# Attention outputs that stay channel-major: transposes on TensorE against a trip through DRAM

## The reference

```python
# L0: RWKV-like mix (shift, two causal scans, sigmoid gate), then one selected 128x128 linear
# L1_attn: 16 heads of 8 channels, full attention over 512 tokens
# L1_ffn:  mixture of 8 experts (hidden 176, top 2) plus a shared one
# L2_attn: 16 heads, rotary, causal
# L2_ffn:  rmsnorm, rotary causal attention with 16 query and 4 key heads, rmsnorm,
#          mixture of 8 experts (hidden 256, top 2)
# L3_attn: 16 query and 4 key heads, causal with ALiBi slopes
# L3_ffn:  layernorm, ternary-quantized 128 -> 512, gelu, layernorm, 512 -> 128
scores = jnp.einsum('bhqd,bhkd->bhqk', Q, K) * scale
attn = jax.nn.softmax(scores, axis=-1)
out = jnp.einsum('bhqk,bhkd->bhqd', attn, V)
out = out.transpose(0, 2, 1, 3).reshape(B, N, D)
return out @ wo.T
```

## Time and profile before

| | us |
|---|---|
| median of 3 runs | 1389.61 |
| lowest and highest | 1388.29, 1390.61 |
| the profiled execution | 1386.62 |
| its span | 1384.8 |
| TensorE busy | 1218.0 (88%) |
| VectorE busy | 932.8 (67%) |
| ScalarE busy | 710.5 (51%) |
| GpSimd busy | 269.9 (19%) |
| mean granted TensorE clock | 0.949 |

### The profile page before, as it was taken

One profiled execution on the slowest core, in us unless ns is written; L12 is line 12 of the kernel. 1 busy time (PEld: TensorE's weight loads), 2 busy tenths in 40 slices (PEclk: granted clock), 3 DMA queues, 4 the chain that ended last, 5 costly groups with the idle time before them and its releaser, 6 DMA issues.

```text
span 1384.8 us, 26785 instructions
## 1 busy us (share of the span) xinstructions
PE 1218.0 (88%) x8190; PEld 650.1 (47%) x8190; DVE 932.8 (67%) x2502; ACT 710.5 (51%) x1300; POOL 269.9 (19%) x557
## 2 busy tenths in 40 slices
PE   3446999999889998999999999999999979999876
PEld 1222233333356655445555555556666535455445
DVE  5877778687455555767778776755554476668676
ACT  2221776777644434566666666663222227666643
POOL 3342211111000012322332332110000211222112
PEclk7557999999999998999999999999999989999988
DMA  7312232310000003323333222100000202221000
GB/s 207 124 65 73 87 90 68 120 35 19 1 1 1 0 1 120 105 66 107 106 98 126 74 78 76 45 4 3 1 0 0 74 12 67 77 81 40 2 1 31
DMA packets 65200, 79.16 MB, mean 57 GB/s; under 512 B 5483, under 2 KB 58068, under 8 KB 64602
## 3 DMA queue, kind: packets, MB, share of 16 engines
q1 hardware_dynamic: 65098, 77.89, 18.1%
HBM read 45.27 MB, written 31.72 MB: 56 GB/s over the span
## 4 chain that ended last, share of the span: by engine, by line
PE 62%; issue 13%; DVE 9%; ACT 4%; DMA 4%; DVEq 3%; POOL 2%; SPq 1%; POOLq 1%; ACTq 0%
PE bank L1606 11%; PE bank L1620 11%; PE bank L1590 9%; PE bank L1772 6%; PE bank L1773 6%; PE bank L1790 5%; PE bank L1574 3%; PE bank L1608 2%; DVE M L1189 2%; DMA KS<-scr_k 2%; PE bank L1640 2%; DVE masked_scores L1186 1%; PE bank L1510 1%; DVE N L1026 1%; PE bank L1570 1%
## 5 line engine op out<-in xcount | busy, mean ns | idle before, releaser
L912 ACT ACTIVATE PT<-bank 128x512 f32<-128x512 f32 (+1 forms) x784 | 427.5, 569 | 246.9 <-PE bank L1608 176.2
L1590 PE MATMUL bank<-KS,QS 125*128 125x512 bf16 (+3 forms) x1024 | 308.6, 329 | 31.5 <-DVE M L1186 12.1
L1606 PE MATMUL bank<-QS,KS 128*128 128x512 bf16 (+3 forms) x1024 | 303.7, 323 | 15.2 <-ACT PT L912 8.0
L1189 DVE TENSOR_REDUCE M<-bank 128x1 f32<-128x512 f32 (+2 forms) x400 | 257.8, 684 | 87.9 <-PE bank L1590 52.2
L1186 DVE CUSTOM_DVE_ANT_0 masked_scores<-bank,maskw 128x384 bf16<-128x384 f32 (+1 forms) x384 | 228.7, 622 | 90.0 <-PE bank L1590 78.8
L1620 PE MATMUL bank<-PT,VA 128*32 128x512 f32 (+3 forms) x2048 | 211.5, 485 | 1.6 <-ACT PT L912 1.0
L1606 PEld LDWEIGHTS bank<-QS,KS 128*128 128x128 bf16 x1024 | 99.3, 98 | 215.5 <-ACT PT L912 152.4
L1590 PEld LDWEIGHTS bank<-KS,QS 125*128 125x128 bf16 x1024 | 100.6, 99 | 109.0 <-DVE M L1189 31.9
L1608 PE MATMUL bank<-identb,maskw 128*128 128x128 bf16 x768 | 147.7, 219 | 0.0
L1790 PEld LDWEIGHTS bank<-MW,PT 128*128 128x128 f32 x864 | 111.7, 193 | 40.8 <-issue 38.2
L1772 PE MATMUL bank<-XT,MW 128*128 128x512 f32 (+1 forms) x232 | 120.7, 602 | 10.1 <-DVE PT L1363 5.9
(11 more groups left out here) (229 smaller groups left out, 1522.6 us busy)
## 6 DMA issues: line engine op xcount, KB each, us to landing
scr_q<-PQ SPq DMA_DIRECT2D x48, 384.0 KB, 3.2
QS<-scr_q SPq DMA_DIRECT2D x64, 288.0 KB
scr_k<-PK SPq DMA_DIRECT2D x24, 384.0 KB, 3.6
KS<-scr_k SPq DMA_DIRECT2D x32, 288.0 KB
QS<-MSB SPq DMA_DIRECT2D x192, 4.0 KB
MW<-in_m_w SPq DMA_DIRECT2D x3, 1024.0 KB, 9.5
MW<-in_m_w SPq DMA_DIRECT2D x3, 832.0 KB
scr_k<-PK SPq DMA_DIRECT2D x24, 96.0 KB, 1.9
```

What stands on the lines that cost most here:

```text
L912: a.activation(PT[kt % 2][:, js[0]:js[-1] + 1, q0:T], tiles(bank[st_bank(L, g, i)][:, 0:w * len(js)], len(js)), ACT.Exp, scale=c["scale"]) ...
L1189: v.tensor_reduce(M[g % 2][:, t * GH + js[0]:t * GH + js[-1] + 1], tiles(bank[S_ORDER[L][i]][:, 0:kl * len(js)], len(js)), AX_X, ALU.max, ...
L1590: r = mm(s, QS[0:ROWS_SHIFT, g * GH + j, t * P:(t + 1) * P], KS[0:ROWS_SHIFT, kv_slot(L, g, j), 0:kl], start=True, stop=not by_pe)
L1606: r = mm(s, KS[:, kv_slot(L, g, j), kt * P:(kt + 1) * P], QS[:, g * GH + j, T - w:T], start=True, stop=not causal)
```

## The change

The output of a unit is never transposed. SP stores `OT` (256 KB) of each unit to a DRAM scratch, `scr_o`, as soon as ScalarE has copied it. When the four units of a block are stored, SP loads the block back twice: the 128 channel rows to `OU`, and the 16 rows of sums, each spread to the 8 rows of its head, to `OS`. VectorE inverts `OS` in place in four pieces of 128 columns, at items 0 to 3 of g=1 in the next block. GpSimd multiplies `OU` with `OS` to `AOT`, and the product with `wo` follows at item 7 of g=1. `o_t`, `o_norm`, `ao_t` and `ao_out` are gone.

```diff
+LAST_R_AT = {2: (0, 1), 3: (2, 3)}
+LAST_Y_AT, LAST_SUM_AT, LAST_NORM_AT, LAST_XT_AT, LAST_OUT_AT = 5, 5, 7, 8, 8
...
-SHIFT_T_AT, O_OUT_AT, O_T_AT, O_NORM_AT, AO_T_AT, AO_OUT_AT = 3, 3, 6, 7, 9, 10
-Y_AT, Y_SUM_AT, Y_STATS_AT = (1, 1), (1, 4), (1, 6)
+SHIFT_T_AT, O_OUT_AT = 3, 3
+RECIP_AT = {(1, 0): 0, (1, 1): 1, (1, 2): 2, (1, 3): 3}
+Y_AT, Y_SUM_AT, Y_STATS_AT = (1, 7), (1, 8), (1, 8)
...
-EARLIER = dict(norm=(2, 1), stats2=(2, 1), norm2=(2, 3), xt=(2, 6), out=(2, 7))
+EARLIER = dict(norm=(2, 2), stats2=(2, 2), norm2=(2, 4), xt=(2, 6), out=(2, 7))
...
-LATE_LOGITS_AT, LATE_GATES_AT, LATE_T_AT = 6, 7, 11
+LATE_LOGITS_AT, LATE_GATES_AT, LATE_T_AT = 9, 9, 12
...
+            def store_o(L, b, g):
+                sp.wait_ge(o_evac, U(L, b, g) + 1)
...
+                    at_least(sp, o_landed, (b + NB * L) * 32)
...
+                sp.dma_start(bass.AP(tensor=scr_o, offset=g * P * T, ap=[[T, P], [1, T]]), OT[:, :]).then_inc(o_stored, 16)
+            def load_o(L, b):
+                B = b + NB * L
+                sp.wait_ge(o_stored, (U(L, b, NG - 1) + 1) * 16)
...
+                sp.dma_start(OS[:, :], bass.AP(tensor=scr_o, offset=HD * T, ap=[[32 * T, H], [0, HD], [1, T]])).then_inc(o_landed, 16)
+                sp.dma_start(OU[:, :], bass.AP(tensor=scr_o, offset=0, ap=[[32 * T, H], [T, HD], [1, T]])).then_inc(o_landed, 16)
...
                     if g == 0:
                         load_stack(L, b, 3)
+                    if g >= 2 and ahead:
+                        load_stack(ahead[0], ahead[1], g - 1)
+                    if prev:
+                        store_o(*prev)
                     if follow:
                         load_shift(*follow)
+                    if end and g == 0:
+                        load_o(*end)
                     if prep:
                         store_parts(*prep)
                         load_stack(*prep, 0)
-                    elif g >= 2 and ahead:
-                        load_stack(ahead[0], ahead[1], g - 1)
                 sequence(L, unit, sp.Fori)
+                if ends_chain(L):
+                    store_o(L, NB - 1, NG - 1)
+                    load_o(L, NB - 1)
...
+            def scale_o(L, b):
+                B = b + NB * L
+                wait(recip_done, (B + 1) * NT)
+                wait(y_ready, b + NB * LAYERS[L]["phase"])
+                g.tensor_tensor(AOT[:, :], OU[:, :], OS[:, :], ALU.mult).then_inc(ao_ready, 1)
...
                     if gg == 1 and end:
+                        scale_o(*end)
                         post_root(LAYERS[end[0]]["phase"], end[1])
...
+            ffn_root(0)
+            scale_o(3, NB - 1)
             post_root(L3_ATTN, NB - 1)
-            ffn_root(0)
+            ffn_root(1)
             post_save(L3_ATTN, NB - 1)
-            ffn_root(1)
...
+            def recip(L, b, i):
+                if i == 0:
+                    dve.wait_ge(o_landed, (b + NB * L + 1) * 32)
+                here = OS[:, i * P:(i + 1) * P]
+                v.reciprocal(here, here).then_inc(recip_done, 1)
```

At the ends of the chains: in both mixtures the four reciprocals stand after chunks 2 and 3 of the first block, `y_out` and `post_sum` with `post_stats` at chunk 5 (into bank 7, no longer bank 6), the norm at 7, the transposes of the result at 8, logits at 9, the gate steps at 9, 10 and 11, and both gate transposes at 12. In the last feed-forward, for VectorE:

```diff
                 if b == 0:
-                    post_sum(L3_ATTN, NB - 1)
+                    for i in range(NT):
+                        recip(3, NB - 1, i)
+                elif b == 1:
+                    post_sum(L3_ATTN, NB - 1, bank[7])
                     post_stats(L3_ATTN, NB - 1)
-                elif b == 1:
-                    post_norm(L3_ATTN, NB - 1)
-                    post_stats2(L3_ATTN, NB - 1)
...
                 if b < NB:
                     ffn_stats(b)
                 if b == 1:
+                    post_norm(L3_ATTN, NB - 1)
+                    post_stats2(L3_ATTN, NB - 1)
                     post_norm2(L3_ATTN, NB - 1)
```

141 lines of the change are left out of this document (61 added, 80 removed).

## The result

The changed kernel takes 1408.52 us (median of 4, 1406.51 to 1409.21); the kernel before took 1390.11 on the same chip (1388.29 to 1391.95). The ratio is 1.013, with a 95% interval of 1.0112 to 1.0148: slower, by 18.4 us, where 10.3 were forecast. Its profiled execution took 1406.51 us, with a span of 1404.7, against a span of 1384.8 before.

A forecast was written before the change was run, and what follows sets the result against it. Inside attention TensorE's own work was taken to set the pace. The terms -32.5 + 30.5 - 3.2 + 4.8 + 4.8 - 1.5 + 6.4 + 1 gave +10.3 us: median 1399.9 us, range 1376 to 1417.

The forecast's parts named there:

- TensorE's gain: Inside attention: dropping the transposes of 61 units and 13 blocks, 0.44 us each, saves 32.5 us, as TensorE is full.
- units g=2 and 3 are 0.44 us shorter: Sign to look for in attention: these units shorten by 0.44 us while TensorE idles about 2 us a block at g=1.
- VectorE at g=1: Attention units g=1 of 13 blocks: reciprocals make VectorE lag and TensorE wait for score banks, +30.5 us (13 to 46).
- the 0.1 us for `y_out`'s wait: At item 7 of g=1: the projection waits about 0.1 us more for GpSimd's multiply behind the fourth reciprocal.
- absorbed by the cheap items behind: At item 8 of a causal g=1: the 2.4 us of sum and statistics together would cost nothing more.
- SP: DMA queue: earlier stack loads remove four KS waits, -3.2 us; output stores delay shift rows at four units, +4.8 (0 to 9).
- Mixtures: First mixture loses 4.8 us (0 to 8) through moved VectorE work and transposes behind the gates; the second gains 1.5.
- Feed-forward: Last feed-forward, VectorE setting the pace: late loads, moved statistics and an uncovered GpSimd root delay the second norm, +6.4 us (2 to 9).
- The banks do not absorb it: Rival: score banks absorb VectorE's lag at g=1, 1.0 us a block, total -7.2, 1382 us; chance 0.27.
- Rows late everywhere: Rival: each store delays shift rows past the next unit by 0.5 us in 48 causal units, +24, 1424 us; chance 0.09.
- the two signs of being wrong: In attention: units g=1 growing by less than 1.1 us, or waits for OS standing on VectorE.
- Hidden edges: Rival: feed-forward and mixture keep their time through unseen slack, -11.2, 1389 us, no difference; chance 0.09.

The follow-up runs named there:

- experiment 8: The kernel before with the four transposes of each unit's output done twice, same result: 1404.65 us, ratio 1.0109.
- experiment 4: The kernel before with four unused 128x128 reciprocals added to VectorE at items 0 to 3 of each block-ending g=1: 1413.07 us, ratio 1.0163.
- experiment 5: The changed kernel with the output projection at item 9 of g=1 instead of 7, sum and statistics at item 10 instead of 8: 1420.08 us, ratio 1.0218.
- experiment 10: Changed kernel, projection at item 9, statistics at 10 of g=1, GpSimd's root behind the split, normalizations later, chains' last blocks as in changed kernel: 1400.36 us, ratio 1.0083.
- experiment 1: The changed kernel with each of the four reciprocals of a block inverting only one column: 1371.86 us, ratio 0.9882.
- experiment 7: The changed kernel inverting compact 128x64 sums before spreading in 13 blocks, with later projection and statistics and reordered last feed-forward: 1422.12 us, ratio 1.0229.
- experiment 9: The changed kernel with compact inversion in ten blocks, GpSimd's multiply behind the split, projection at g=2, normalizations at g=3: 1412.95 us, ratio 1.0189.
- experiment 12: The compact inversion in ten blocks with projection at g=2, plus SP's spreading load moved behind the shift rows: 1398.59 us, ratio 1.0066.
- experiment 11: The changed kernel with SP issuing the shift rows ahead of the store of the output in every unit: 1421.99 us, ratio 1.0244.
- experiment 3: The changed kernel with only the order of VectorE's and GpSimd's work in the last feed-forward changed: 1405.70 us, ratio 1.012.
- experiment 2: The kernel before with only SP's stack loads of g=2 and 3 issued ahead of the shift rows: 1382.56 us, ratio 0.9964.

## Why the prediction was right, and where its size was off

The direction and the mechanism held, and 1408.5 lies in the range; but the range, 1376 to 1417, was wide enough to hold a faster kernel too. The sum was 8 us short by the medians (10.3 of 18.4) and 9.7 by the profiles: the units g=1 took 6.7 more than forecast, the feed-forward 1.5, the start 1.4 by scatter. The mixtures nearly cancel. Outside g=1 the total came out within 0.8, by luck: the transposes gave some 6 us less than forecast, and the stores cost some 4 less.

**TensorE's gain: too large by some 6 us.** "TensorE is full there" was read from two units and applied to 61. Experiment 8 adds what two thirds of them would. Outside g=1, the changed kernel won 23.4 us. Of these 3.2 are the KS waits and 0.7 the last block, whose wait of 2.44 for the normalized rows became 1.74 where +1 was forecast; the first block of layer 1 lost 1.0 on MSB. That leaves about 20.5 for the transposes, against 26.8. The sign "units g=2 and 3 are 0.44 us shorter" held at g=3 (0.27 to 0.44, more where a KS wait went too); the 13 units g=2 behind a block's end won 1.3 us together, not 5.7.

**VectorE at g=1: 37 instead of 30.5** (if the transposes gave their 5.7 there). The lag of the reciprocals was sized at 29 (2.2 a causal block); experiment 4 gives 24 by adding them, 1.9 a block. The 939 ns of one confirm the line through the earlier trace rows, as do the 542 ns of 128x64 (6.25 ns an element from 252 gives 552). The step that failed is the 0.1 us for `y_out`'s wait: "behind reciprocal 3" GpSimd ends 1.26 us after the fourth reciprocal, which itself is late by the lag, and TensorE meets it at item 7 in each of the 13 blocks, 10.3 us in waits and 13.2 in unit time (experiment 5), where the sum had 1.0. That I had taken TensorE to be as late as VectorE at item 7 is my reading of the slip: it is ahead by what the banks absorb.

**Sum and statistics at item 8, "absorbed by the cheap items behind": not quite.** In the units of layer 2 shown above, the waits of 0.49 for M and 0.48 for the split at the start of g=2 are theirs: both are there with the reciprocals cut to a column as well (0.50 and 0.48). GpSimd's root for these statistics stands ahead of the split. Experiments 5 and 10 show how near this was: two items later the same work costs 31 us in g=2, and 6 once GpSimd splits first, the two normalizations come later and three blocks go back.

**The estimate worked out from the Trainium skill** (VectorE: DVE Perf Modes, "First, the fixed hardware budget"), 1.07 us for 128 elements by a repeat count of 8, is off: 939 ns, with all fixed time in it.

**SP: -3.2 right, +4.8 not realised.** KS waits went from 7.9 us in 5 to 4.9 in 1. MSB went from 4.0 to 4.3. The stores are not free: in the first block of layer 1, whose g=1 has no reciprocals, the wait for MSB grew from 1.46 to 2.43 us, 1.0 of the 1.2 forecast. In the next two blocks (0.89 and 0.32 before) it is gone, covered by the stalls of g=1. Where the stalls shrink (experiment 1) MSB rises to 7.4. So the two terms could not be added: the one hides the other. That each DMA engine takes the descriptors of a ring in order (DMA: Bandwidth & Descriptors, "Queues, rings and completion order", in the Trainium skill) agrees with the small stores of experiments 7, 9 and 12, which land just behind the parts issued ahead of them; no run separates it from engines that are merely shared. In experiment 11 what held things up was SP waiting, not a transfer.

**Mixtures: +3.5 and -2.3 over all profiles, against +4.8 and -1.5.** The waits for the gates' transposes are there, 4.36 and 1.91 us at 415.60 and 418.32. No run varied the places in the first mixture alone, so which of its moves costs how much stays open.

**Feed-forward: +7.9 against +6.4.** The second `ffn_norm` came 32.2 us behind the copy, as forecast (32), and experiment 3 prices the uncovered root at 2.3 (2.7 in the sum). The 1.2 us behind that norm were not in the sum; four other profiles with this order have 73.1 to 73.5 us behind the last copy instead of 74.0, so most of it is there each time.

**The rivals.** The banks do not absorb it: 2.9 us a block, over the 1.55 from which that rival decides, though experiment 4 shows them absorbing half of the reciprocals. Rows late everywhere: three waits for MSB, not 48. Of the two signs of being wrong, growth under 1.1 us at g=1 did not come (2.4 a block, the transposes' gain included); a wait for OS inside attention came once, 0.47 us in layer 2's last block, too little to matter. Hidden edges: the feed-forward and the first mixture lost what was forecast or near it.

## What to carry to other kernels

An engine that looks full in two units need not be so in sixty: doubling the work that is to go (experiment 8) costs one run and tells where it is hidden, if not to the last us. When an operation is moved to an in-order engine, follow what is queued behind it: here a multiply and a root each cost more through their followers than by themselves. Twice a new order behind it won most of a loss back (20 us in experiment 10, with two normalizations moved along, and 14 in experiment 12). And when a queue stands still, list everything that it waits for there: the transfer issued last in experiment 9 added 0.2 us to a wait that stood there anyway. And a wait removed uncovers the next one, so terms for waits in the same stage don't add.

## What the hardware showed unasked

A stall of TensorE costs again afterwards. In experiment 5 a stretch of 4 us with 0.5 us of matmuls was followed by more than 4 us at a granted clock of 0.50 (1.2 GHz) and a return within the 2 us after 840; the same matmuls then took 12.40 us of busy time instead of 9.70. In experiment 10 a single wait of 1.68 us at the same place left the clock at 1.00, but in experiment 2 a single wait of 2.04 us, which ended at 636.11, was followed by 0.51 in the next 2 us and 0.64 in the 2 us after. So two waits, each short, with a matmul between them can cost what a longer one does.

And the time of a small transfer depends on what was issued ahead of it. The 32 KB store of the inverted sums landed after 1.45, 1.48 and 1.82 us in the three blocks of experiment 7 where no stores of parts stand ahead of it. Behind the parts it took up to 3.48 (experiment 12), and in all 30 such blocks of experiments 7, 9 and 12 it landed 0.16 to 0.66 us behind the last part. The 64 stores of 256 KB of OT in the changed kernel have a median of 2.0. In experiment 9 one us of the store's 3.2 lay where the DMA engines were full (share 1.02, not the 98% of my expectation for experiment 12), two where they were nearly idle.
